# Attention values on 32 by 32 parts of the TensorE array in both layers, the first layer's values projected in the token stage and placed through memory

## The reference, cut to what matters

```python
f = fftshift(fft2(images)); power_sorted = abs(crop(f))[..., idx]      # 16 rings by radius
tokens = einsum('bnf,ef->bne', rings(power_sorted), W) + b             # 64 x 16 x 192
h = concatenate([cls, tokens], 1) + pe                                 # 64 x 17 x 192
qkv = h @ W_attn + b_attn                                              # 12 heads of 16
out = softmax(causal(q @ k.T / 4)) @ v                                 # per image and head, 17 x 17
h = layernorm(h + out @ W_proj + b_proj)
...                                                                    # second attention, not causal, no bias
out = softmax(q @ k.T * 16 ** -0.5) @ v
...                                                                    # then 8 experts, top 2, and a last layernorm
```

## Time and profile before

| what | us |
|---|---|
| median of 3 runs (826.88 to 835.3) | 830.22 |
| the profiled execution | 831.77 |
| its span, first to last instruction | 830.0 |
| PE busy in the span | 715.0 |
| DVE / ACT / POOL busy | 533.1 / 443.6 / 427.9 |

### The profile page before, as it was taken

The page is one execution under the profiler, slowest core; times in us unless marked ns, Lnnn a source line. Parts: engine busy times, 40 slices in busy tenths (PEclk is TensorE's granted clock), DMA queues, the critical chain, the costliest instruction groups (busy, mean ns, idle before and its releaser), DMA issues. The chain is left out here.

```text
span 830.0 us, 17940 instructions
## 1 busy us (share of the span) xinstructions
PE 715.0 (86%) x6425; PEld 623.9 (75%) x6425; DVE 533.1 (64%) x1058; ACT 443.6 (53%) x864; POOL 427.9 (52%) x375
## 2 busy tenths in 40 slices
PE   4999999999999902579898889999899988999980
PEld 4888888888888802578788778776567767999980
DVE  3788888888888711356555555588759774555543
ACT  1778878778787831334444444343264231666640
POOL 3667666666666435377777777200300022567751
PEclk9999999999999956689999999999999975999995
DMA  9855448964788449555555555310000576233324
GB/s 233 220 150 153 132 139 232 242 184 133 194 236 231 197 95 210 191 157 164 152 143 152 147 149 152 101 38 2 1 1 2 230 216 187 44 58 57 55 29 125
DMA packets 78516, 114.85 MB, mean 138 GB/s; under 512 B 8791, under 2 KB 58108, under 8 KB 78076
## 3 DMA queue, kind: packets, MB, share of 16 engines
q1 hardware_dynamic: 61246, 76.80, 33.2%
q0 software_dynamic: 14336, 35.40, 16.6%
q10 hardware_dynamic: 2880, 1.90, 0.7%
HBM read 91.83 MB, written 22.25 MB: 137 GB/s over the span
## 5 line engine op out<-in xcount | busy, mean ns | idle before, releaser
L592 PE MATMUL psum<-power,tT 128*128 128x192 f32 x864 | 160.2, 341 | 65.8 <-DVE tT L719 65.2
L592 PEld LDWEIGHTS psum<-power,tT 128*128 128x128 f32 x864 | 145.8, 197 | 77.5 <-issue 41.7
L533 POOL DMA_INDIRECT rows<-power_table,rank_row x144 | 145.5, 1010 | 66.1 <-issue 54.3
L327 PE MATMUL ps<-dft,fold 112*112 112x97 f32 x1536 | 168.0, 264 | 10.9 <-POOL fold L294 10.9
L327 PEld LDWEIGHTS ps<-dft,fold 112*112 112x112 f32 x1536 | 167.3, 180 | 11.4 <-issue 10.8
L719 DVE SCALAR_TENSOR_TENSOR tT<-rows,swaps,scaled 128x384 f32<-128x384 f32 x144 | 82.7, 616 | 119.1 <-ACT scaled L647 118.8
L647 ACT ACTIVATE scaled<-rows,swaps 128x384 f32<-128x384 f32 x144 | 80.6, 607 | 138.1 <-DMA rows<-power_table,rank_row 138.1
L301 POOL TENSOR_TENSOR ss<-uv 97x388 f32<-97x388 f32 x96 | 82.2, 877 | 97.1 <-ACT uv L367 97.1
L399 DVE TENSOR_TENSOR folded<-ps,far 112x388 f32<-112x388 f32 x192 | 98.4, 553 | 46.7 <-ACT far L355 46.5
L294 POOL TENSOR_TENSOR fold<-img 112x896 f32<-112x896 f32 x48 | 103.4, 2154 | 14.8 <-DMA img<-in_x 8.7
L416 DVE TENSOR_TENSOR uv<-ps,odd 97x388 f32<-97x388 f32 x192 | 97.7, 549 | 2.6 <-ACT odd L360 2.6
(11 more groups left out here) (174 smaller groups left out, 933.9 us busy)
## 6 DMA issues: line engine op xcount, KB each, us to landing
img<-in_x SPq DMA_DIRECT2D x48, 784.0 KB, 5.2
power_table<-power SPq DMA_DIRECT2D x16, 576.0 KB
power<-in_w_tok SPq DMA_DIRECT2D x3, 1728.0 KB, 10.2
power<-in_w SPq DMA_DIRECT2D x8, 579.0 KB, 7.6
power<-in_w SPq DMA_DIRECT2D x4, 1152.0 KB, 10.8
rows<-power_table,rank_row POOLq DMA_INDIRECT x144, 3.1
power_table<-power SPq DMA_DIRECT2D x1, 1200.0 KB
power_table<-power SPq DMA_DIRECT2D x1, 1072.0 KB, 15.1
```

The source lines that it names most:

```text
L327: last = pe.matmul(ps1[0:HALF, j % 2, i, col:col + FREQ], fold[:, j // UPG % FOLD_RING, part, x0:x0 + HALF], dft[:, part * FREQ:(part + 1) ...
L533: pool.indirect_dma_start(out=rows[:, j % RING, half, :], out_offset=None, in_=table[0:RECORDS if j % CHUNKS < PLAIN else RECORDS + P * (L ...
L592: last = pe.matmul(ps[:, q % 2, 0:DIM], points[:, j % SWAPPED, c, s].rearrange("p h b -> p (h b)"), wt[:, c, s, chunk, :], start=(chunk == ...
```

## The change

The values of both layers are no longer made block-diagonal. Each probability matrix (17 by 17 for an image and a head) meets its own 17x16 values on a 32 by 32 part of the array: row group i holds head 4m+i of a set of four heads, column group r holds image r of four. `values` becomes 96 matmuls a unit with 17 rows, 32 columns and 16 moving columns, for which `p_transposes` makes 6 transposes of 128x128 in place of 4, of probabilities padded to 32 keys a head. `own_values` and `place_v` are gone in both layers, with the constants `spread` and `own_v`. The columns of the value weights are sorted on the host so that each row group's heads lie together.

Layer 1 projects its values straight onto the four row groups: 64 matmuls a unit of 96 rows by 32 columns with 48 moving columns, in place of 4 of 96x128 with 192.

Layer 0's values are projected in the token stage (`project`, two matmuls more a batch), copied by ACT (`batch_v`), stored by SP in `value_rows` and brought to their 32-partition places by 204 small DMAs (`place_values`: 9 batches, 12 DMAs for each of the 17 positions). `store_tokens` comes after all of these in SP's queue, and values(0) waits for the last of them (`v_in`). The second copy of the tokens into `xT` is gone. Three banks hold the output projection in place of four, one tile in place of four goes ahead of values(7), and values come before p_transposes in PE's order.

```diff
+    def place_values(sp):
+        for b in range(PAIRS + 1):
+            first, count = positions_of(b)
+            sp.wait_ge(v_set, b + 1)
+            sp.dma_start(v_rows[first * BATCH:(first + count) * BATCH, :], v_turn[0:count * BATCH, b % 2, :]
+                         ).then_inc(v_stored, 16)
+            sp.wait_ge(v_stored, 16 * (b + 1))
...
+            for s in range(first, first + count):
+                for i in range(LANES):
+                    for images, place in W["v_places"]:
+                        n = images.stop - images.start
+                        sp.dma_start(place[i * LANE + s:i * LANE + s + 1],
+                                     v_rows[None, s * BATCH + images.start:s * BATCH + images.stop,
+                                            i * V_COLS:(i + 1) * V_COLS]).then_inc(v_in, 16)
     def store_tokens(sp):
+        place_values(sp)
...
+            for vb in (0, 1) if b == 1 else (b,) if b > 1 else ():
+                at_least(pe, v_set, vb - 1)
+                n = positions_of(vb)[1] * BATCH
+                for h in range(2):
+                    last = pe.matmul(ps[0:n, V_BANK + vb % 2, 0:DIM], batchT[0:KH + h, vb % 2, h, 0:n], W["wv"][0:KH + h, h, :],
+                                     start=(h == 0), stop=(h == 1))
             last.then_inc(batch_mm, 1)
...
-            act.activation(lanes_at(first, count), part.rearrange("p h (s b) -> p h s b", b=BATCH), ACT.Copy)
...
+        def batch_v(b, j):
+            first, count = positions_of(b)
+            n = count * BATCH
+            act.wait_ge(batch_mm, b + 1 if j else 2)
+            at_least(act, v_stored, 16 * (b - 1))
+            act.activation(v_turn[0:n, j % 2, :], ps[0:n, V_BANK + j % 2, 0:DIM], ACT.Copy).then_inc(v_set, 1)
...
         def project_v(u):
...
+            for n in range(UI):
+                first = (u * UI + n) * LANE
                 for h in range(2):
+                    for i in range(LANES):
+                        last = pe.matmul(psum[i * LANE:(i + 1) * LANE, V_BANK, n * V_COLS:(n + 1) * V_COLS],
+                                         xT[0:KH, h, first:first + LANE],
+                                         W["wv"][:, h, i * V_COLS:(i + 1) * V_COLS], start=(h == 0), stop=(h == 1))
             last.then_inc(v_mm, 1)
...
         def values(u):
             pe.wait_ge(pT_done, u + 1)
+            if L1:
+                pe.wait_ge(v_out, u + 1)
+            elif u == 0:
+                pe.wait_ge(v_in, 16 * SEQ * LANES * len(B["v"]))
             at_least(pe, o_done, u)
+            for m in range(TURNS):
+                g, hh = m // HSETS, m % HSETS
+                for i in range(LANES):
+                    keys = slice(i * LANE, i * LANE + SEQ)
                     for r in range(LANES):
+                        v, n = values_of(image(u, g, r))
+                        last = pe.matmul(psum[r * LANE:(r + 1) * LANE, VALUE_BANK + i, m * HEAD:(m + 1) * HEAD],
+                                         pT[keys, u % 2, m, r * LANE:(r + 1) * LANE],
+                                         v[keys, n, hh * HEAD:(hh + 1) * HEAD], start=True, stop=True)
             last.then_inc(av, 1)
...
-        by_units([(1, scores), (0, project_v), (1, own_values), (2, p_transposes), (3, values), (4, o_transposes)],
-                 out_projection)
+        by_units([(1, scores)] + [(0, project_v)] * L1 + [(3, values), (2, p_transposes), (4, o_transposes)], out_projection)
...
-        by_units([(1, mask_and_max), (2, sums), (1, place_v), (3, share_out)])
+        by_units([(1, mask_and_max), (3, share_out), (2, sums)])
```

184 lines of the change are left out of this document (99 added, 85 removed).

## The result

| what | before | after |
|---|---|---|
| median, us | 831.16 (826.88 to 835.3, 4 runs) | 921.41 (918.04 to 922.93, 4 runs) |
| span of the profiled execution, us | 830.0 | 919.5 |
| mean granted clock of TensorE | 0.938 | 0.868 |
| PE instructions | 6425 | 9821 |
| PE busy, us | 715.0 | 752.7 |

The ratio is 1.108 (95% interval 1.102 to 1.115). The forecast was 832.8 us with a range up to 852: the change costs 90 us where I had 2.6.

A forecast was written before the change was run, and what follows sets the result against it. PE was taken to bound the attentions, with POOL pacing the token stage. Layer 0's late values (+4.3 us) and layer 1's gain (-1.7) summed to +2.6 on 830.22, giving 832.8 us, range 821 to 852.

The forecast's parts named there:

- X: Time of a unit's new values matmuls: 192 pairs at 6.5 ns plus 0.16, 1.41 us; other end 4.0 us.
- What bounds the kernel: POOL paces the token stage; PE bounds both attentions at 5.12 us a unit, with DVE just behind at 4.69.
- Layer 0's unit, 3.65 us: Layer 0 attention: kept steps and transposes 2.24 us plus values X of 1.41, in place of 5.12; 6.2 at the other end.
- gone and kept: Layer 0's unit: project_v 1.50 and own_values 0.84 us go; scores 0.84, o_transposes 0.57 stay, p_transposes become 0.83.
- a long run is paced by the supply of instructions: Rival on PE's small matmuls: a pair costs 10 ns or more, giving 843 us, or 884 at 20 ns; chance 0.27.
- Layer 1's unit, 5.09 us: Layer 1 attention: 2.24 + 1.41 + project_v 1.44 us, in place of 5.12; 8 units give 0.2 us.
- The clock: PE restarting after over 10 us of standing still at values(0) runs at a lower clock: 1.5 us added.
- v_in, 560.0: Layer 0's last value loads land at 560.0 us behind SP's issue and two stores, so values(0) waits on PE.
- c = 0.48: SP's time to issue one small value load, 0.48 us; plausible bounds 0.36 to 0.55.
- The token stage: Extra projections are hidden by POOL's pace; tokens end up to 0.6 us later within scores(0)'s slack: 0 in the sum.
- The ends of the layers: One projection tile instead of four ahead of values(7): values(7) comes 2.1 us earlier, 0.6 given back.
- From v_in on, 25.4 + 1.5 us: Layer 0 from v_in to values(7)'s end: PE's remaining work 25.4 us plus 1.5 for the clock, ending at 586.9.

The follow-up runs named there:

- the bench: Kernel before, 7 wide matmuls at layer 0's end replaced by four forms of 256 small-column matmuls written out one after the other; whole kernel 1000.4 us.
- chop6_turning: Kernel before, each values matmul cut into 6 of 16 columns, taking the four column groups in turn, no row groups; 896.9 us, ratio 1.076.
- bench_loop: Kernel before, 7 wide matmuls at layer 0's end replaced by four matmul forms, each 8 turns of a hardware loop of 32 matmuls; 988.3 us.
- the looped version: Changed kernel, most small matmuls from the second unit on coming from hardware loops that repeat the first heads and first image, other values left out; 903.7 us.
- the first looped form: In the kernel before with four looped matmul forms added: 17 rows by 32 columns going round all 16 array parts; 512 pairs in 6.94 us.
- the forms on one part and on the whole array: Two forms written out in the kernel before, 17 by 32 on one array part and 128 by 128; 50 and 207 ns a pair.
- chop6: Kernel before, each values matmul of 96 moving columns cut into 6 of 16 that follow each other, no row groups; 900.7 us, ratio 1.080.
- after_early_values: Changed kernel, layer 0's values in two places instead of three, 136 loads instead of 204, last batch's store and loads on ACT's queue; 914.2 us.

## Why the prediction was wrong, step by step

**In short.** The step that failed is the one to the unit's time, 2.24 + X: it prices the kept steps at the full clock, prices a pair of X by the start of a run (6.5 ns), and has no term for the rate at which written-out instructions arrive. The runs showed 27 to 29 ns a pair beyond the first 200 or so, and 1.2 GHz for most of the units.

**What bounds the kernel.** Right for the kernel before. In the changed kernel PE still leads the attentions, but it is itself held up by its instructions; POOL paced the token stage.

**Layer 0's unit, 3.65 us: wrong, it was 7.45.** The mechanism "gone and kept" was right, and three terms were not. The kept steps, 2.24 us at full clock, took 3.84 at 1.2 GHz (1.51 + 1.34 + 0.99): +1.6. The values X, forecast at 1.41, took 3.61 - 1.41 = 2.20 (583.15 to 586.76, less the gap): +0.8. The gap: +1.4. Together the 3.8 that were missed.

**X.** I chose 6.5 ns a pair from the first 12 starts of a run over the 20 ns of a whole run. A burst makes 9.2 to 9.8 ns at the full clock (217 pairs in 1.99 us in the bench, 128 in 1.25 from 695.12 in the changed kernel) and 10.6 to 11.2 at the lower (192 in 2.04 from 569.32, 128 in 1.43 from 683.76), and that lasts for what is already there. A long row of written-out pairs makes 27 to 29 ns. My own rival named it, "a long run is paced by the supply of instructions", with 843 us at 10 ns and 884 at 20. But I priced it within the run, and even its upper price didn't reach. What it needed was a count for the whole unit against a rate of supply, and no row of before showed that rate, since 58 ns a pair never reached it. The range ended at 852 because I cut the pair price at 11 ns: this step made the range too narrow. The evidence against it was weak: those runs were explained by their columns, and a limit that nothing has met leaves no trace.

**The rule that would have helped** stands in the Trainium skill (Runtime: NRT & Kernel Launch, Instruction fetch mechanics), and I hadn't weighed it. It says that instructions arrive in blocks of 16 KB, 256 of them; the traces agree, at 16 KB a packet and 128 pairs between gaps. It also says that fetching is hidden, because the sequencer issues more slowly than the blocks come. Here the measurement decides against it: PE issued an instruction each 4.6 ns (9.2 / 2), a block came each 3.45 to 3.73 us, which is 13.5 to 14.6 ns an instruction. Its advice to write code out fails for such rows too: 11.76 us written out, 6.94 from the loop.

**Layer 1's unit, 5.09 us: wrong, 11.0.** The kept steps took 1.36 + 1.33 + 1.00 = 3.69 in place of 2.24, +1.4; `project_v` 2.42 in place of 1.44 (691.83 to 694.25, at 1.2 GHz), +1.0; the gaps 0.51 + 2.48 = 3.0; the values 4.92 less the gaps, 1.93 in place of 1.41, +0.5. With 5.09 that makes 11.0. Like for layer 0, the sum was right where it said what work there is, and had no term for supply and clock.

**The clock.** I gave it 1.5 us, once, for the restart behind the wait. It costs 1.4 to 1.7 us in each unit at 1.2 GHz. How much of the 90 us is clock and how much is gaps can't be split cleanly, since the clock fell behind a gap (chop6_turning), fell in light work without one (bench_loop), and slower work at the low clock hides part of the gaps. With most of the gaps gone the looped version still loses 70 us (903.7 against 833.9 for the kernel before in the same round), with 15 ns and more a pair from its loops. Light work alone is enough to bring the clock down, as the first looped form and layer 1 of the looped version show, and the forms on one part and on the whole array, where PE was busy throughout at 0.50. How much the long wait adds to it in layer 0 is open.

**v_in, 560.0: too early by 9.3 us, of which 4.35 are the profile's late token stage and 5 the path's own.** The mechanism was right and the size off. A load costs 0.66 us, over the upper bound of 0.55: 48 x 0.18 = 8.6 us more than c = 0.48. Against that the store took 1.7 us to the first load and not 2.6, twice, the last landing 1.4 and not 2.3, and the last copy came about 0.9 sooner. In sum +5, and 564.97 when the profile's 4.35 us of the token stage are taken off.

**The token stage: right.** 0 was forecast, and the value path added to the kernel before leaves the stage's end where it was; the 4.35 us of the profiled execution are within what one execution differs from another.

**The ends of the layers: half right.** values(7) comes 2.0 us earlier in the kernel before (2.1 forecast), but 1.3 are given back, not 0.6. In the changed kernel the tail of layer 0 grew by 3.6 us at the lower clock.

**From v_in on, 25.4 + 1.5 us** to the end of values(7): 54.0 were measured, all by the unit's terms.

## What to carry to other kernels

Count the instructions of a stretch, and not only their time: written-out PE code that asks for a pair of weight load and matmul faster than each 28 ns over more than about 200 pairs will wait for its own code, and the idle time stands in the trace as "issue". A change that trades few wide matmuls for many small ones is to be priced by the number of pairs per unit against this rate, and then once more at half the clock. And where a step is moved to another queue, look at what that queue does next: the loads on ACT held up the first exponent.

## What the runs showed of the hardware

- Instructions come to PE in packets of 16 KB, 256 instructions. At the gaps of the changed kernel PE goes on 2.2 to 3.0 us after the start of a packet; from piece to piece it is 3.45 to 3.73 us. About 205 to 217 pairs run through at first.
- A loop of 64 pairs took no packet within a form and makes 13.1 to 13.6 ns a pair; the loops of 32 pairs in the looped kernel's values make 15 to 18 at the lower clock. A burst of written-out code makes 9.2 to 9.8 at the full clock and 10.6 to 11.2 at the lower.
- PE's clock fell from 1.00 to 0.50 in a run of 512 small pairs without a gap (bench_loop, 592 to 598 us).
- A pair in a row of twelve on the same 32 columns costs 24.7 ns at the full clock (chop6), one in a row of 512 costs 50 at the lower, a pair on 128 columns 207 ns at the lower, with 16 moving columns in each case. With the four column groups in turn, two pairs on each, the bound is gone, and row groups on top give nothing more (13.6 against 13.1 ns).
- A gap of 2.08 us was followed by 34 us at 1.2 GHz (555.6 to 589.7 in chop6_turning), in the last 22 of which PE had no wait.
- SP issues a load of 8 to 32 pieces of 192 bytes in 0.51 to 0.75 us, ACT one of 28 or 36 in 0.73 to 0.79 for nine in a row and up to 1.66 for the seven before them (after_early_values).
